# Feed-forward weights of an S5-type block: scratch kept in bf16 and loaded by SyncE, output stores issued by GpSimd

## What is computed

```python
x = x + layernorm(ssm(layernorm(x)))     # ssm: B projection to 256 states x 2, a linear scan over time, C projection, + x*D
x = x + layernorm(ffn(layernorm(x)))
# ffn: h = gelu(x @ bw1.T + b1); out = h @ bw2.T + b2
# bw = mean(|w|, axis=1) * sign(w): binarized weights, w1 is [4096, 1024], w2 is [1024, 4096]
```

## Time and profile before

| | us |
|---|---|
| time, median of 2 runs | 4107.71 (4069.2 and 4146.23) |
| profiled execution | 4077.46 |
| its span, slowest core (7) | 4075.6 |
| spans of the 8 cores | 4058.7 to 4075.6 |
| PE busy, share of the span | 2413.6, 59% |
| VectorE, ScalarE, POOL busy | 1503.2, 1401.1, 309.7 |
| DMA moved | 686.65 MB, mean 168 GB/s |

### The profile page before, as it was taken

How to read it: one execution, slowest core, us unless ns; L and a number is a source line. 1 busy time by engine, 2 the same in 40 slices (tenths; PEclk the granted TensorE clock), 3 DMA queues, 4 the chain that set the end, 5 groups by cost and what they waited for, 6 DMA issues and landing times.

```text
span 4075.6 us, 44232 instructions; the slowest of 8 cores (4058.7 to 4075.6 us)
## 1 busy us (share of the span) xinstructions
PE 2413.6 (59%) x14412; PEld 1454.7 (36%) x14412; DVE 1503.2 (37%) x3300; ACT 1401.1 (34%) x2149; POOL 309.7 (8%) x580
## 2 busy tenths in 40 slices
PE   0000003685858586858676777677676768585967
PEld 0000001353525353535343444444443435352534
DVE  1000027526161616262524343343435352616132
ACT  4530001333343333333333333434343333333343
POOL 0001100010101010101010000000000101010100
PEclk9999998797879797979888888888887979797978
DMA  6687321272626263626363545445453636262735
GB/s 197 196 184 118 69 52 52 99 263 83 255 97 250 111 240 114 256 94 249 123 227 135 203 169 196 176 177 195 156 216 134 238 114 258 94 257 81 273 135 204
DMA packets 185971, 686.65 MB, mean 168 GB/s; under 512 B 78825, under 2 KB 91279, under 8 KB 118930
## 3 DMA queue, kind: packets, MB, share of 16 engines
q0 software_dynamic: 90240, 562.08, 38.2%
q1 hardware_dynamic: 86802, 88.19, 7.8%
q10 hardware_dynamic: 8704, 33.56, 2.1%
HBM read 339.84 MB, written 58.72 MB: 98 GB/s over the span
## 4 chain that ended last, share of the span: by engine, by line
PE 41%; DVE 21%; issue 14%; DMA 14%; ACT 9%; DVEq 1%; ACTq 0%; POOLq 0%; SPq 0%; POOL 0%
PE pb L946 19%; PE pcA L963 11%; PE pcB L963 10%; DMA sx<-x 2%; DVE sx L837 2%; ACT tt L834 2%; DVE u L732 2%; DMA scr_a<-a2col 2%; ACT L953 2%; DMA scr_w2b<-n1tm 1%; DMA scr_w1b<-n1tm 1%; ACT gel L953 1%; DVE dtm L703 1%; DVE ys L744 1%; DVE u L742 1%
## 5 line engine op out<-in xcount | busy, mean ns | idle before, releaser
L946 PE MATMUL pb<-n2fm,w1s 128*128 128x256 bf16 x8192 | 1150.8, 288 | 107.1 <-DVE u L758 75.3
L946 PEld LDWEIGHTS pb<-n2fm,w1s 128*128 128x128 bf16 x8192 | 844.2, 103 | 488.1 <-issue 184.3
L953 ACT ACTIVATE gel<-pb,b1col,a1col 128x256 bf16<-128x256 f32 x1024 | 569.0, 563 | 1303.0 <-PE pb L946 1302.2
L963 PE MATMUL pcA<-w2s,gel 128*128 128x512 bf16 x2048 | 669.3, 411 | 512.4 <-ACT gel L953 505.9
L963 PE MATMUL pcB<-w2s,gel 128*128 128x512 bf16 x2048 | 664.2, 408 | 14.9 <-DVE mo L1003 14.9
L963 PEld LDWEIGHTS pcA<-w2s,gel 128*128 128x128 bf16 x2048 | 198.6, 102 | 585.0 <-issue 557.5
L411 PE MATMUL pcA<-amo,outb 1*128 1x512 f32 x2 | 2.0, 1122 | 550.2 <-DMA amo<-scr_a 550.2
L963 PEld LDWEIGHTS pcB<-w2s,gel 128*128 128x128 bf16 x2048 | 213.0, 104 | 304.1 <-issue 99.1
L925 POOL DMA_DIRECT2D w1s<-scr_w1t x256 | 135.3, 529 | 2306.6 <-PE pb L946 2306.6
L752 PE MATMUL pb<-n1fm,cB 128*128 128x512 bf16 x512 | 180.2, 522 | 90.6 <-DVE u L758 74.3
L662 ACT ACTIVATE junk<-sx 128x1024 bf16<-128x1024 f32 x64 | 67.6, 1056 | 449.9 <-DVE cC L571 384.2
(11 more groups left out here) (303 smaller groups left out, 2469.4 us busy)
## 6 DMA issues: line engine op xcount, KB each, us to landing
w1s<-scr_w1t POOLq DMA_DIRECT2D x256, 1024.0 KB, 4.6
w2s<-scr_w2t POOLq DMA_DIRECT2D x256, 1024.0 KB, 5.2
sx<-x ACTq DMA_DIRECT2D x32, 1024.0 KB, 8.4
outb<-w SPq DMA_DIRECT2D x32, 512.0 KB, 4.6
tt<-w SPq DMA_DIRECT2D x32, 512.0 KB, 5.9
out<-outb SPq DMA_DIRECT2D x32, 512.0 KB, 4.6
out<-amo SPq DMA_DIRECT2D x32, 512.0 KB, 3.6
scr_w1b<-n1tm POOLq DMA_DIRECT2D x8, 1024.0 KB, 7.3
```

The source lines that it names most:

```text
L946: pe(lambda e, k=k, bk=bk, wr=wr, hbq=hbq, hf=hf: e.matmul(pb[bk][:, 0:256], w1s[wr][:, k * 512 + hbq * 128: k * 512 + hbq * 128 + 128], n ...
L953: act(lambda e, hb=hb, bk=bk, gs=gs: e.activation(gel[gs][:, :], pb[bk][:, 0:256], AF.Gelu, bias=b1col[:, hb:hb + 1], scale=a1col[:, hb:hb ...
L963: pe(lambda e, hb=hb, mg=mg, ng=ng, wr=wr, gs=gs, hbq=hbq: e.matmul(pcm[mg][:, ng * 512:(ng + 1) * 512], gel[gs][:, mg * 128:(mg + 1) * 12 ...
```

## The change

The two transposed scratch tensors become bf16, so their writes and the weight loads no longer cast. The 512 weight loads go to the `sp` queue, the 64 output stores to the `gp` queue. Two lambdas bind `c0` and `c1` as default arguments. Buffers, sizes in SBUF and the places in the code at which each DMA is emitted stay as they are.

```diff
--- before.py
+++ after.py
@@ -127,8 +127,8 @@
     d_out = nc.dram_tensor("out", [SEQS, L, H], F32, kind="ExternalOutput").ap()
     s_w1b = nc.dram_tensor("scr_w1b", [HF, H], BF16, kind="Internal").ap()
     s_w2b = nc.dram_tensor("scr_w2b", [H, HF], BF16, kind="Internal").ap()
-    s_w1t = nc.dram_tensor("scr_w1t", [8, 128, HF], FP8, kind="Internal").ap()
-    s_w2t = nc.dram_tensor("scr_w2t", [8, 128, 4 * H], FP8, kind="Internal").ap()
+    s_w1t = nc.dram_tensor("scr_w1t", [8, 128, HF], BF16, kind="Internal").ap()
+    s_w2t = nc.dram_tensor("scr_w2t", [8, 128, 4 * H], BF16, kind="Internal").ap()
     s_a2 = nc.dram_tensor("scr_a2", [8, 128], F32, kind="Internal").ap()
 
     es = ExitStack()
@@ -855,8 +855,8 @@
                 reads=["wt2", "wt1"], writes=["wt2"])
             dve(lambda e: e.tensor_scalar(wt2[:, c0:c1], wt2[:, c0:c1], EPS, None, ALU.add, ALU.bypass),
                 reads=["wt2"], writes=["wt2"])
-            act(lambda e: e.activation(wt2[:, c0:c1], wt2[:, c0:c1], AF.Sqrt), reads=["wt2"], writes=["wt2"])
-            dve(lambda e: e.reciprocal(st2[:, 12 + c0:12 + c1], wt2[:, c0:c1]), reads=["wt2"], writes=["st2.rs"])
+            act(lambda e, c0=c0, c1=c1: e.activation(wt2[:, c0:c1], wt2[:, c0:c1], AF.Sqrt), reads=["wt2"], writes=["wt2"])
+            dve(lambda e, c0=c0, c1=c1: e.reciprocal(st2[:, 12 + c0:12 + c1], wt2[:, c0:c1]), reads=["wt2"], writes=["st2.rs"])
             dve(lambda e: e.tensor_tensor(st2[:, 8 + c0:8 + c1], st2[:, 8 + c0:8 + c1], st2[:, 12 + c0:12 + c1], ALU.mult),
                 reads=["st2.nm", "st2.rs"], writes=["st2.nm"])
 
@@ -922,7 +922,7 @@
             if NPIECE_TOTAL is not None and g >= NPIECE_TOTAL[0]:
                 return
             piece, wr = g % 8, g % 2
-            dma("gp", lambda e, piece=piece, wr=wr: e.dma_start(
+            dma("sp", lambda e, piece=piece, wr=wr: e.dma_start(
                 out=w1s[wr][:, :], in_=s_w1t[piece, :, :]),
                 reads=["s_w1t"], writes=[f"w1s{wr}"], sem=f"dw1{wr}")
 
@@ -930,7 +930,7 @@
             if NPIECE_TOTAL is not None and g >= NPIECE_TOTAL[0]:
                 return
             piece, wr2 = g % 8, g % 2
-            dma("gp", lambda e, piece=piece, wr2=wr2: e.dma_start(
+            dma("sp", lambda e, piece=piece, wr2=wr2: e.dma_start(
                 out=w2s[wr2][:, :], in_=s_w2t[piece, :, :]),
                 reads=["s_w2t"], writes=[f"w2s{wr2}"], sem=f"dw2{wr2}")
 
@@ -1018,7 +1018,7 @@
                 dve(lambda e, m=m, mg=mg, xt=xtiles[m]: e.tensor_tensor(outb[mg][:, :], xt, tt[mg][:, :], ALU.add),
                     reads=[xres[m], f"tt{mg}"], writes=[f"outb{mg}"])
                 tok_tile = c * 4 + mg
-                dma("sp", lambda e, s=s, tok_tile=tok_tile, mg=mg: e.dma_start(
+                dma("gp", lambda e, s=s, tok_tile=tok_tile, mg=mg: e.dma_start(
                     out=d_out[s].rearrange("(a p) d -> p a d", p=128)[:, tok_tile, :],
                     in_=outb[mg][:, :]),
                     reads=[f"outb{mg}"], writes=[], sem=f"do{mg}")
```

## The result

The changed kernel takes 1.0185 times as long as the one before, 95% interval 1.0143 to 1.0228: clearly slower, but whether by less or by more than 2% stays open. It ran 11 times, the kernel before 10 times. Its profiled execution took 4140.37 us (span 4138.8 on core 7), 63 us more than that of before. The forecast was 4074 us with a range up to 4140; the median of all runs is 4153.6.

The account below looks back on a forecast made before the run. TensorE was taken to wait mainly for ScalarE's GELU, with weights 1.5 us from late and the second-half x load setting the pace. Against 4077.46 us, -3 - 2 + 1 + 1 = -3 gave 4074 us, range 4040 to 4140.

Parts of the forecast that it names:

- The slack of the weights (part 1): Loop weight loads on SP: still 2.9 us of engine time, landing 5.5 us, slack 1.5 growing to 1.9 us; worth 0.
- The x load (part 1, third step): Second-half x load beside nearly two weight loads: -0.2 us x 14 = -3 us, bounds -11 and +39 us.
- The rule on HBM: Stretch of the x load moves 369 GB/s, above about 358: 3% longer, 0.2 us x 14 = 3 us.
- The setup (part 2): Setup scratch writes without a cast: -2 us; bounds -30 us, and +15 us each for scr_w1t and scr_w2t.
- Parts 3 and 4: First four weight loads behind C_mat on SP: +1 us; 64 stores moved to POOL: +1 us.
- (a): Rival: loop weight loads become the bound above 3.48 us of engine time each; 4176 us, chance 0.12.
- Its milder form: Of (a): loads at 3.2 to 3.5 us, only x load and stray late loads pay; 4090 to 4140 us, chance 0.18.
- (b): Rival: setup and x load gain in full, -30 - 11, 4036 us; chance 0.04.
- (c): Rival: POOL's software queue was starved of descriptors by VectorE and SP frees it; at most 114 us, 3963; chance 0.02.

Follow-up runs that it names:

- e5: Changed kernel with all weight loads after the first two pieces copied on SP from constant SBUF tiles instead of HBM; x waits 110 us, loop 3364.5 us.
- e8: Changed kernel with each scratch piece stored as two blocks of 128 x 2048 (4 KB rows); x waits 103 us, w2t stage 132.5 us, loop 3361 us.
- e1: Kernel before with only the two scratch tensors made bf16, weight loads staying on POOL and stores on SP; ratio 1.0204.
- e3: Kernel before with the second-half x load issued at hidden block 8 instead of 16; ratio 0.9871.

## Why the prediction was wrong

**The slack of the weights (part 1): nearly right.** It took 2.9 us of engine time for 1.05 MB with and without the cast, from the share of q0 over the whole span, in which the writes of the setup are contained. In the loop alone (core 7, 1000 to 3800 us, before and changed) the weight queues read:

```profile
q0 software_dynamic: 61356, 446.82, 43.1%
...
q1 hardware_dynamic: 59904, 436.23, 45.7%
```

That is 2.83 us and 3.08 us for a load, and 2.80 and 3.01 in the median of the cores: a plain load costs 0.2 us more than a casting one, where "no change" was taken. The slack held nearly everywhere; late weights grew from 2.0 to 8.8 us, which I had at 0. The landing "stays at 5.5 us" was wrong: over the whole loop the medians rose by 1.3 and 1.7 us to 5.9 and 6.9. e5 ties that to HBM. The stated doubling to 608 MB was read (608.27).

**The x load (part 1, third step): the step that failed.** It took -0.2 us for each of 14 loads, -3 us in all. Measured: 44 us more x waits. The step held fixed what runs beside the x load, nearly two weight loads, and priced only their engine time. But the measured price (3.01 us instead of 2.80) gives by the step's own sum some 0.6 us for a load, less 0.2 to 0.4 for the earlier start: about a tenth of the 44 us. What changed is the overlap. Before, 91% of x had started before the load behind it came, and 0.45 MB of that load was moved by x's last packet. In the changed kernel x has started only 41% by then, and the whole 1.05 MB comes between its packets; its last packet is at 9.96 us instead of 6.41. In the runs on POOL this goes with how much the weight loads read, which the change doubled, and not with their engine time. The +39 us that I gave as upper end, from a price of 3.83 us, came near the size by luck: that price never held.

**The rule on HBM** (the Trainium skill, HBM Reference, Specifications: about 358 GB/s for a core when both of a pair stream) would have given 3 us. The runs don't bear out even this as the mechanism: during an x load the changed kernel moved 297 GB/s, below that figure, and e5 without HBM reads for weights had no shorter x waits.

**The setup (part 2): wrong in one half.** The writes into `scr_w1t` came out a little better than said (11.1 to 10.6 us on one buffer, 11.2 to 9.4 on the other, where 0.23 us was taken off each). Those into `scr_w2t` I had as a bound of +15 us and took as nothing; their stage grew by 21.5 us, beyond that bound, and the setup by 16.5. The step priced bytes alone; e8 shows the same bytes in 132.5 us with rows nearer together.

**Parts 3 and 4: right.** C_mat landed after 6.93 us instead of 7.46 with the weight loads queued behind it. The stores landed after 7.0 and 7.8 us instead of 4.6 and 3.6, and no engine shows a wait for them.

**The rivals.** (a) named the right sign and the x load as its second term, but put the bound at 3.48 us of engine time for a load, and the loads never came near it. Its milder form (only the x load and stray late loads pay, 4090 to 4140 us, given 0.18) is the picture that was measured, though it asked for 3.2 to 3.5 us a load and 3.01 were paid. (b) and (c) did not occur: e1 against the changed kernel (1.0204 and 1.0185, intervals overlapping) shows nothing won by leaving POOL. On the rule behind (c) (the Trainium skill, SBUF - State Buffer, Who interferes with whom) this case has no sign of starved descriptors: the same uncast loads landed after 5.9 and 6.6 us from POOL (e1) and 5.9 and 6.9 from SP, and x waits were shorter with the weights on POOL than on SP in all three pairs.

**The expectation behind e3 had the same fault as the prediction**: it took a wait away and did not ask what is late next. The x load moved into a stretch where the weights have 1.5 us of slack.

What stays open: why x's packets are slower beside plain weight loads even while they are nearly alone, and why SP's queue adds some 9 us in one pair and 33 in another. Part of the latter is seen: the load behind is issued 0.67 us after the x load on SP and 1.1 us after it on POOL. That it is the load behind that makes x late is read from the order of the packets; no run leaves out that load alone. Whether the distance of the written rows is the cause in the setup, or the length of contiguous runs that goes with it in e8, was not separated.

## What to carry to other kernels

Before a transfer is made "cheaper", look for the one load that something waits for at once, and price the change on that load: here 14 of 1 MB, the x loads of the second halves, carried nearly all of what 512 hidden ones did to the loop. Ask too what is issued right behind it: a load that starts a little later or moves a little slower can have all of the next one between its packets. A cast in the DMA is not only a cost: it halves what is read, and here the load that came behind it on the same engines landed sooner. If such a load is on the path, move its issue first; that was worth more (0.9871, and 0.9742 with the sums spread) than any choice of queue or type.

## What the runs showed of the hardware

- A casting load (FP8 to bf16, 0.5 MB read, 1 MB written) occupied the DMA engines for 2.80 us and a plain one of 1 MB on the same queue for 3.04, and a 1 MB load behind them was waited for 62 against some 97 us in 14 waits (both on POOL). Behind plain loads of 0.5 MB (1.72 us) it was 64 us.
- The last packet of that x load came 6.41 us after its issue in the kernel before and 9.96 us in the changed one, though the first came after 2.41 and 2.46 us: the next weight load had moved 0.45 MB by then in the one case and all of its 1.05 MB in the other.
- The weights' source in HBM or SBUF changed the landing of 1 MB on SP from 5.9 and 6.9 us to 4.5 and 5.0, and did not shorten the waits for x (106 and 110). On POOL it did shorten them, from 62 to 47 us with the cast and from some 97 to 77 without.
- Issuing the same copies from SP instead of POOL lengthened the waits for an x load on ScalarE's queue in three pairs: some +9, +15 and +33 us over 14 waits.
- 32 writes of 128 rows of 2 KB into HBM took 150 us with rows 8 KB apart and 132.5 with rows 4 KB apart (each behind a transpose).
